# The first context pair ahead of the rows in both attention loops, and the waits for the expert output moved to the gather

## The reference

```python
x = x + tanh(g_xattn[0]) * xattn_0(layernorm(x), ctx, ...)       # 16 heads of 16
x = x + tanh(g_ffn[0])   * moe_0(layernorm(x), ...)              # 8 experts, one per row, fixed capacity
x = x + tanh(g_xattn[1]) * xattn_1(layernorm(x), ctx, ctx, ...)
x = x + tanh(g_ffn[1])   * moe_1(layernorm(x), ...)              # 4 experts, best two of each row
```

## Time and profile before

| | us |
|---|---|
| median of 3 runs | 2115.59 (2114.24 to 2116.48) |
| the profiled execution | 2114.74 |
| its span | 2112.6 |

### The profile page before, as it was taken

One profiled execution on the slowest core, in us unless ns is written; L12 is line 12 of the kernel. 1 busy time (PEld: TensorE's weight loads), 2 busy tenths in 40 slices (PEclk: granted clock), 3 DMA queues, 4 the chain that ended last, 5 costly groups with the idle time before them and its releaser, 6 DMA issues.

```text
span 2112.6 us, 57359 instructions
## 1 busy us (share of the span) xinstructions
PE 2019.0 (96%) x19532; PEld 1772.0 (84%) x19532; DVE 1760.6 (83%) x4918; ACT 1479.2 (70%) x3172; POOL 1201.8 (57%) x1736
## 2 busy tenths in 40 slices
PE   6999999999699999999699999999999999999997
PEld 5878888887599999999578887888788888888885
DVE  5888888888588888888588888888589999999996
ACT  4766666666487878787366666666578888888885
POOL 5778888887200000000377777777357777777776
PEclk9999999999799999999899999999999999999998
DMA  7565222221466666666422222222101100011000
GB/s 243 171 198 169 69 72 64 69 74 38 162 244 222 245 228 239 229 235 238 153 59 76 69 74 69 74 69 77 39 24 31 31 31 30 31 31 30 30 27 18
DMA packets 168047, 226.09 MB, mean 107 GB/s; under 512 B 20454, under 2 KB 152170, under 8 KB 157420
## 3 DMA queue, kind: packets, MB, share of 16 engines
q1 hardware_dynamic: 161644, 205.99, 29.5%
q0 software_dynamic: 6144, 16.79, 2.6%
HBM read 153.77 MB, written 68.94 MB: 105 GB/s over the span
## 4 chain that ended last, share of the span: by engine, by line
PE 87%; DVE 5%; issue 3%; DMA 2%; POOL 1%; ACT 1%; SPq 0%; POOLq 0%; ACTq 0%; DVEq 0%
PE ps L1281 11%; PE ps L1297 11%; PE ps L1041 10%; PE ps L1000 8%; PE ps L1081 5%; PE ps L1127 5%; PE ps L1241 4%; PE ps L1227 4%; PE ps L1148 4%; PE ps L1158 3%; PE ps L1181 3%; DVE nmax L1434 3%; PE ps L1060 3%; PE ps L1075 2%; PE ps L1098 2%
## 5 line engine op out<-in xcount | busy, mean ns | idle before, releaser
L1434 DVE TENSOR_REDUCE nmax<-ps 128x16 f32<-128x2048 f32 x128 | 292.8, 2287 | 32.6 <-PE ps L1098 32.2
L889 ACT ACTIVATE prob_t<-ps 128x2048 f32<-128x2048 f32 x128 | 240.8, 1881 | 102.4 <-PE ps L1081 102.4
L694 POOL COPY slot_in<-slot_all 128x1 int32<-128x1 int32 x64 | 13.3, 207 | 473.4 <-DMA eo_d<-eo 473.4
L1041 PE MATMUL ps<-w2f,a_t 128*128 128x256 f32 x1024 | 231.7, 379 | 0.3 <-ACT a_t L811 0.3
L1281 PE MATMUL ps<-xgt_hi,w_hl 128*128 128x256 f32 x1248 | 230.6, 283 | 1.0 <-DVE xgt_lo L1701 1.0
L1297 PE MATMUL ps<-w_hl,hid_hi 128*128 128x256 f32 x1248 | 226.9, 284 | 0.0
L1041 PEld LDWEIGHTS ps<-w2f,a_t 128*128 128x128 f32 x1024 | 189.6, 190 | 23.8 <-ACT a_t L811 0.6
L961 ACT ACTIVATE hid<-ps,b_in 128x256 f32<-128x256 f32 x312 | 145.8, 468 | 83.5 <-PE ps L1281 68.0
L1281 PEld LDWEIGHTS ps<-xgt_hi,w_hl 128*128 128x128 f32 x1248 | 196.0, 190 | 1.4 <-issue 1.4
L811 ACT ACTIVATE a_t<-ps,be_in,g_in 128x128 f32<-128x128 f32 x512 | 185.6, 469 | 12.3 <-PE ps L1060 11.4
L1297 PEld LDWEIGHTS ps<-w_hl,hid_hi 128*128 128x128 f32 x1248 | 191.5, 188 | 0.0
(11 more groups left out here) (237 smaller groups left out, 6306.8 us busy)
## 6 DMA issues: line engine op xcount, KB each, us to landing
w_raw<-in_w_dram SPq DMA_DIRECT2D x78, 1024.0 KB, 6.8
c_t<-in_ctx_in_dram SPq DMA_DIRECT2D x128, 128.0 KB, 3.4
x_d<-x SPq DMA_DIRECT2D x128, 128.0 KB, 1.7
slots_d<-zeros SPq DMA_DIRECT2D x12, 1024.0 KB, 5.5
eo_d<-zeros SPq DMA_DIRECT2D x12, 1024.0 KB, 5.2
xg<-slots_d SPq DMA_DIRECT2D x39, 256.0 KB, 2.8
eo_d<-eo SPq DMA_DIRECT2D x39, 256.0 KB, 2.2
x_in<-in_x_dram SPq DMA_DIRECT2D x64, 128.0 KB
```

The lines of the kernel that those rows point to most:

```text
L889: nc.scalar.activation(prob_t[:].rearrange("p a k -> p (a k)"), scores.rearrange("p a k -> p (a k)"), ACT.Exp, scale=SOFT).then_inc(y["exp ...
L1041: mm = pe.matmul(dst, a_t[:, b.parity, e, c, :], w2f[:, e, c, :], start=False, stop=True, skip_group_check=True)
L1434: nc.vector.tensor_reduce(nmax[:, b.parity, :, 0:4], scores.rearrange("p a (r k) -> p a r k", k=P), AX_X, ALU.max, negate=True).then_inc(y ...
```

## The change

It does these things:

1. In both loops SP loads the first context pair in step -5, ahead of any rows; `c_hi` and `c_lo` of it are made in step -5, k is projected and copied in step -3. From then on the context load stands ahead of the row load in a step.
2. Only `wk_hi` and `wk_lo` are split ahead of the steps. `wv_hi` and `wv_lo` are split at the end of step -2 (on VectorE behind the statistics of batch 1), and TensorE waits for them only ahead of v.
3. SP's wait for the last two expert stores is gone. POOL's stands behind the first copy to `slot_in`, ahead of the first gather. `slot_in` has memory of its own (4 words; two constants of the layout move by 4).
4. In step 67, at the end of loop 0, POOL makes the low part of the last attention output (`o_lo`) ahead of `rstd` of batch 62, and VectorE makes the slot numbers of batches 56 to 59 in step 67 and no longer in step 68.

```diff
@@ SyncE @@
-                    b = s + 4
-                    if b.within(B):
-                        ...
-                        sp.dma_start(x_in[:, b.off % 12, :], row(x_src, b)).then_inc(y["x_came"].of(b), 16)
-                    e = s + 3
-                    if e.off % 2 == 0 and e.within(B):
+                    e = At(0, 0) if s.off == -LEAD else s + 3
+                    if (s.off == -LEAD or e.off > 0) and e.off % 2 == 0 and e.within(B):
                         if (e - 3).begun:
                             sp.wait_ge(y["c_lo_done"].of(e - 3), y["c_lo_done"].at(e - 3))
                         for t in range(2):
                             b = e + t
                             sp.dma_start(c_t[:, e.off // 2 % 2, :, t, :], row(ctx_in, b).rearrange("p (c k) -> p c k", c=C))\
                                 .then_inc(y["c_came"].of(b), 16)
+                    b = s + 4
+                    if b.within(B):
+                        ...
+                        sp.dma_start(x_in[:, b.off % 12, :], row(x_src, b)).then_inc(y["x_came"].of(b), 16)
...
-                    for g in (NH - 2, NH - 1):
-                        sp.wait_ge(z["eo_stored"].of(At(0, g)), z["eo_stored"].at(At(0, g)))
@@ GpSimd @@
+                    if (s - 4).within(B) and not (s - 3).within(B):
+                        low_part()
+                        second_rstd()
+                    else:
+                        second_rstd()
                     b = s + 5
                     if n == 1 and b.within(B):
                         ...
                         nc.gpsimd.tensor_copy(slot_in[:, b.off % 4, :], token(slot_all, b)).then_inc(y["slot_read"].sem, 1)
                         pool.wait_ge(y["slot_read"].of(b), y["slot_read"].at(b))
+                        if b.off == 0:
+                            for g in (NH - 2, NH - 1):
+                                pool.wait_ge(z["eo_stored"].of(At(0, g)), z["eo_stored"].at(At(0, g)))
...
+                    if not ((s - 4).within(B) and not (s - 3).within(B)):
+                        low_part()
...
-                    e = s + 2
-                    if e.off % 2 == 0 and e.within(B):
+                    e = At(0, 0) if s.off == -LEAD else s + 2
+                    if (s.off == -LEAD or e.off > 0) and e.off % 2 == 0 and e.within(B):
                         r = e.off // 2 % 3
                         pool.wait_ge(y["c_hi_done"].of(e + 1), y["c_hi_done"].at(e + 1))
                         nc.gpsimd.tensor_tensor(c_lo[:, r], c_t[:, e.off // 2 % 2], c_hi[:, r], ALU.subtract)\
...
-                    for g in (NH - 2, NH - 1):
-                        pool.wait_ge(z["eo_stored"].of(At(0, g)), z["eo_stored"].at(At(0, g)))
@@ ScalarE @@
-                nc.scalar.activation(wv_hi[:], w_vp[:], ACT.Copy).then_inc(s_wv[n], 1)
...
-                    e = s + 2
-                    if e.off % 2 == 0 and e.within(B):
+                    e = At(0, 0) if s.off == -LEAD else s + 2
+                    if (s.off == -LEAD or e.off > 0) and e.off % 2 == 0 and e.within(B):
...
-                    e = s + 1 if s.off == -1 else s
+                    e = At(0, 0) if s.off == -3 else s
...
+                    if s.off == -2:
+                        act.wait_ge(s_wv[n], 2)
+                        nc.scalar.activation(wv_hi[:], w_vp[:], ACT.Copy).then_inc(s_wv[n], 1)
@@ TensorE @@
-                pe.wait_ge(s_wv[n], 4)
+                pe.wait_ge(s_wv[n], 2)
...
-                    e = s + 1 if s.off == -1 else s
+                    e = At(0, 0) if s.off == -3 else s
...
                     e = s - 1
                     if e.off % 2 == 0 and e.within(B):
+                        if e.off == 0:
+                            pe.wait_ge(s_wv[n], 4)
@@ VectorE @@
-                dve.wait_ge(s_wv[n], 2)
-                nc.vector.tensor_tensor(wv_lo[:], w_vp[:], wv_hi[:], ALU.subtract).then_inc(s_wv[n], 1)
+                dve.wait_ge(s_wv[n], 1)
                 nc.vector.tensor_tensor(wk_lo[:], w_k[:], wk_hi[:], ALU.subtract).then_inc(s_wv[n], 1)
...
+                    if n == 0 and b.off % CH == 0 and b.within(B) and b.off != B - 2 * CH:
+                        slots_from_places(b)
...
                         nc.vector.tensor_reduce(den8[:], ex8[:], AX_X, ALU.add).then_inc(st.sem, 1)
+                        if b.off == B - 2 * CH:
+                            slots_from_places(b)
...
+                    if s.off == -2:
+                        dve.wait_ge(s_wv[n], 3)
+                        nc.vector.tensor_tensor(wv_lo[:], w_vp[:], wv_hi[:], ALU.subtract).then_inc(s_wv[n], 1)
```

44 lines of the change are left out of this document (23 added, 21 removed).

## The result

The changed kernel takes 2126.63 us (median of five, 2126.38 to 2127.30) against 2114.39 for the kernel before in the same comparison (2114.17 to 2116.48): a ratio of 1.0051, 95% interval 1.0040 to 1.0062. It is slower by 12.2 us, where 3.7 were to be gained. The profiled execution took 2126.62, its span 2124.7.

What follows compares the result with a forecast made beforehand. TensorE was taken to bound the long middles, so only three seams could move: 0.8 + 0.4 + 2.5 = 3.7 us off the profiled 2114.74 gives 2111.0, as a median 2111.9. Range 2110.0 to 2116.2.

Steps and rivals of the forecast that it cites:

- nothing in the change touches an instruction of these stretches: Long middles of both attention loops, expert loop and last part: TensorE-bound and untouched, so only three seams can move.
- Start of loop 0, 0.8 us gained: Loop 0's first seam: early k lets q start 0.9 us earlier, less 0.1 for a late context pair.
- The waiting context: Loop 0, context pair 4, 5: lands 5 us later behind the bulk, at about 30.0, just hidden; 0.1 us taken.
- End of loop 0, 0.4 gained: Last scatters of loop 0: early `o_lo` brings at most 0.7 us to the last chunk; bounds -0.3 and 0.8.
- the step that the prediction named: End of loop 0: the fifth of the last eight scatters needs the last chunk's slot numbers, so can't begin before 549.65.
- Start of loop 1, 2.5 gained: Loop 1's first batches: `xh` of batch 3 takes 0.41 us in place of 2.86, bringing 2.5 us.
- 5 us, the bulk just behind it: Start of loop 1: bulk weights issued just behind gather 4, which then flies 5 us in place of 6.95.
- the gap: Start of loop 1: 0.9 us before gather 6 starts on POOL, in which `xh` of batch 3 gets through.
- rival (a): Start of loop 1: `xh` of batch 3 waits for gather 6, `km_r` and `qm` again; 2115.7, chance 0.20.
- (b): Early k frees nothing: late pair 4, 5 takes loop 0's gain, POOL paces loop 1; 2115.2, chance 0.15.
- (c): Start of loop 1: late context holds POOL at the first `c_lo`, every gather behind it; 2117.6, chance 0.05.
- A time slower beyond the noise: Whole kernel: a time over 2119.8, from a mishap only; chance 0.04.

Runs made afterwards that it cites:

- e10: The kernel before with only layer 1's bulk weights issued in step 4 of loop 1 in place of step 2: 2110.95 us, ratio 0.9989.
- e9: The changed kernel with slot numbers ahead of `nmax_x` again and layer 1's bulk weights held until step 4 of loop 1: 2117.71 us, ratio 1.0017.
- e13: e9 with GpSimd's first `c_lo` of loop 1 back in its old step, behind three gathers: 2114.79 us, ratio 0.9999.
- e7: The changed kernel with slot numbers ahead of `nmax_x` again and unread matmuls filling TensorE's two gaps at loop 0's start: 2118.72 us, ratio 1.0014.

## Why the prediction was wrong, point by point

**What bounds the kernel.** The reading of before was right, the conclusion from it wrong: "nothing in the change touches an instruction of these stretches". That sentence was not read from the diff line by line. This is the step of the prediction that failed: it put at nothing what the diff does to the chunk steps of loop 0, where the order of two blocks on VectorE changed. It left out a term of 11.3 us that is larger than all the others together. And its price was in the rows: `xh` at 2.86 us in the earlier trace rows, held by three GpSimd operations, was in the prediction as a rival for one instruction of one seam, while the eight of each chunk were moved next to the same three.

**Start of loop 0, 0.8 us gained.** `k_in` ended at 14.7 (forecast 14.5) and q of batch 0 started at 16.81 (16.9): the schedule was right. The step that failed is behind it. Durations of q and v were taken from the earlier trace rows as constants, and they hang on what TensorE did before. q of batch 1 took 1.92 in place of 1.06, v 2.9 us in place of 1.7 (22.96 to 25.9, 22.97 to 24.65), and `nmax` of batch 1 came 0.64 late. Over the seven traces with the new start and no fill, against the six with the old one, the term is -0.3 in place of +0.8. The waiting context was sized rightly: `c_hi` of pair 4 started at 29.86, forecast 30.

**End of loop 0, 0.4 gained.** Counted from `nmax` of batch 63, the last scatter starts at 33.26 in place of 33.84, 0.58 earlier, and the fifth one, at 561.02, waited 1.84 us for VectorE's numbers, the step that the prediction named. To the last `eo` it is 503.9 in the mean of twelve traces against 504.3 in five: 0.4, the term of the sum. But single traces of the twelve reach from 502.9 to 504.6, those of the five from 504.0 to 504.5, so it is in keeping with the traces and not shown by them. The first scatter came 2.3 earlier (554.18 less the shift of 11.87, against 544.58), as said, and as said the fifth one sets the end.

**Start of loop 1, 2.5 gained.** It lost 0.7 in the mean of the traces, 1.1 in the profiled pair. The context landed early, `c_lo` ended at 1041.88, in the kernel before's time (less 10.48) 1031.4 where 1032.7 was forecast, and `km_r` of batch 0 moved by 0.5 and not 1.3. Both were better than forecast. The step that failed is the flight of gather 4: "5 us, the bulk just behind it". The bulk went out at 1051.36, the gather at 1051.37, and it flew 6.70 us, 6.95 in the earlier trace rows. Against the forecast the gather was 0.8 us early and the bulk 1.7, since X was: the bulk had been placed 0.9 behind the gather, and came with it. So `xh` missed the gap and rival (a) occurred. The prediction took any start ahead of gather 6 for safe, and (a) took the flight alone for the key. In the old start that is nearly so: e10 took the bulk away, and `xh` got through. In the new one it isn't: e9 took it away too, and the sum of batch 4 was caught by the same block of GpSimd operations. There the order of `c_lo`, gathers and masks on GpSimd loses the gap even with a flight of 3.5 us, as e13 shows, in which `xh` took 0.41.

**The sum.** In the two profiled executions: +0.55 at the start of loop 0, +11.3 in its middle, -1.4 to the last `eo`, +1.1 at the start of loop 1 make +11.6, and the spans differ by 12.1. The last 0.5 us lie behind the marks and were not looked into.

**Rivals and chances.** (b)'s mechanism occurred in e7, where nothing else hid it. (c), GpSimd held at the first `c_lo`, didn't: it waited 0.29 us for it. A time slower beyond the noise had 0.04, for want of the one mechanism that was in the diff.

## What to carry to other kernels

Before costing a moved block, write down for each engine the order of calls before and after, also for blocks that the diff seems only to wrap in a function: the place of a call is part of the change. In this kernel a short VectorE operation was cheap only where GpSimd paused; beside a run of long GpSimd operations three of eight were each held for about one of them. So count how many operations can meet such a run, and not only their own nanoseconds. Whether they meet can turn on 14 ns, so look at such a place in more than one trace. And an operation that got earlier on TensorE made what follows slower here, since it left the engine idle between, while a bulk load one queue wait further back was worth more than a whole rearranged start.
